# Mamba convolution: the running sum of the taps kept in the projection's PSUM banks, and the head's steps renumbered around it

## What is computed

```python
xz = jnp.einsum("bld,ed->ble", x, in_w)
xb, z = jnp.split(xz, 2, axis=-1)
xc = depthwise_conv(xb, cw)              # 4 taps, causal
xb = silu(xc + cb)
dbc = einsum("ble,re->blr", xb, xp_w)    # delta, B, C
...
v = BETA * v + mi_t                      # scan over the tokens
h = dA_t * h + v
y_t = einsum("ben,bn->be", h, C_t)
...
y = (y + dp * xb) * silu(z)
out = einsum("bld,ed->ble", y, ow)
```

## Time and profile before

| | us |
|---|---|
| median of three runs | 4340.58 |
| the profiled execution's own time | 4348.82 |
| its span (first to last instruction) | 4347.0 |
| PE busy | 3439.8 (79%) |
| DVE busy | 2853.4 (66%) |
| POOL busy | 2088.3 (48%) |
| ACT busy | 1959.2 (45%) |

### The profile page before, as it was taken

One profiled execution on the slowest core, in us unless ns is written; L12 is line 12 of the kernel. 1 busy time (PEld: TensorE's weight loads), 2 busy tenths in 40 slices (PEclk: granted clock), 3 DMA queues, 4 the chain that ended last, 5 costly groups with the idle time before them and its releaser, 6 DMA issues. The chain is left out here.

```text
span 4347.0 us, 70779 instructions
## 1 busy us (share of the span) xinstructions
PE 3439.8 (79%) x20348; PEld 2281.5 (52%) x20349; DVE 2853.4 (66%) x4863; ACT 1959.2 (45%) x4196; POOL 2088.3 (48%) x1206
## 2 busy tenths in 40 slices
PE   6888878954888888888874888888888873599980
PEld 4454545633555555555542555555555543488870
DVE  3444442335887888888865887888888867655545
ACT  1212111214666666666634666656666643233320
POOL 0101000012767767676762776767676665422216
PEclk8787877976999999999986999999999995699995
DMA  1000000011221323122221222313222115211113
GB/s 51 0 0 0 0 9 13 0 57 32 68 63 49 79 51 76 51 67 62 51 67 33 63 66 52 78 52 75 55 56 74 51 52 176 87 46 48 46 41 109
DMA packets 151529, 228.95 MB, mean 53 GB/s; under 512 B 25106, under 2 KB 83890, under 8 KB 149556
## 3 DMA queue, kind: packets, MB, share of 16 engines
q1 hardware_dynamic: 143156, 202.30, 17.4%
q0 software_dynamic: 8064, 23.08, 1.8%
HBM read 119.99 MB, written 23.59 MB: 33 GB/s over the span
## 5 line engine op out<-in xcount | busy, mean ns | idle before, releaser
L895 POOL TENSOR_TENSOR m_hc<-m_h,m_Cb 128x1024 f32<-128x1024 f32 x512 | 1212.2, 2370 | 635.2 <-DVE m_h L1019 358.1
L1019 DVE TENSOR_TENSOR_SCAN m_h<-m_dA,m_hlast,m_bank 128x256 f32<-128x256 f32 x2048 | 1348.2, 726 | 143.2 <-PE m_bank L1300 92.4
L1283 PE MATMUL m_bank<-m_hc,ident 128*128 128x512 f32 x2048 | 1145.0, 648 | 85.3 <-POOL m_hc L895 84.7
L1148 ACT ACTIVATE m_dA<-m_delta,m_rate 128x256 f32<-128x256 f32 x2048 | 881.5, 500 | 25.7 <-DVE m_h L1019 23.1
L1298 PE MATMUL m_bank<-m_M,m_U 128*128 128x128 bf16 x4096 | 607.0, 226 | 215.0 <-DVE m_h L1019 175.0
L1298 PEld LDWEIGHTS m_bank<-m_M,m_U 128*128 128x128 bf16 x4096 | 409.9, 101 | 453.0 <-DVE m_h L1019 301.6
L1300 PE MATMUL m_bank<-m_M,m_U 112*128 112x128 bf16 x4096 | 608.2, 226 | 0.0
L1300 PEld LDWEIGHTS m_bank<-m_M,m_U 112*128 112x128 bf16 x4096 | 414.8, 101 | 197.8 <-issue 169.8
L1283 PEld LDWEIGHTS m_bank<-m_hc,ident 128*128 128x128 f32 x2048 | 331.6, 200 | 138.2 <-POOL m_hc L895 102.7
L965 DVE SCALAR_TENSOR_TENSOR m_cv<-m_xpre,m_conv,m_cv 128x256 f32<-128x256 f32 x384 | 344.5, 938 | 23.1 <-ACT m_cv L1085 18.6
L1213 PE MATMUL m_bank<-m_pair,m_in 128*128 128x256 f32 x1024 | 266.5, 386 | 8.3 <-ACT m_cv L1085 4.6
(11 more groups left out here) (273 smaller groups left out, 5534.6 us busy)
## 6 DMA issues: line engine op xcount, KB each, us to landing
m_Cb<-m_c_rows SPq DMA_DIRECT2D x256, 256.0 KB, 3.3
m_M<-m_Mhi SPq DMA_DIRECT2D x128, 256.0 KB, 4.4
m_M<-m_Mlo SPq DMA_DIRECT2D x64, 256.0 KB, 3.7
m_U<-m_Uhi SPq DMA_DIRECT2D x128, 128.0 KB, 3.4
y_rows<-x_y SPq DMA_DIRECT2D x40, 256.0 KB, 2.1
m_U<-m_Ulo SPq DMA_DIRECT2D x64, 128.0 KB, 3.6
g_stage<-in_e_w SPq DMA_DIRECT2D x8, 1024.0 KB, 5.4
o_stage<-in_e_w SPq DMA_DIRECT2D x16, 512.0 KB, 4.0
```

Source lines behind the costliest of these rows:

```text
L895: nc.gpsimd.tensor_tensor(hc[:, g].rearrange("p m a t -> p m (a t)"), h[:, p % 2, 2 * g:2 * g + 2].rearrange("p m a t -> p m (a t)"), Cb[: ...
L1019: nc.vector.tensor_tensor_scan(h[:, p % 2, m, a, :], dA[:, p % 2, m, a, :], VB[m][:, a * CM:(a + 1) * CM], hlast[:, NG * p + a, m:m + 1], ...
L1148: nc.scalar.activation(dA[:, p % 2, m, a, :], delta[:, par, m, :], ACT.Exp, scale=rate[:, m, NG * p + a:NG * p + a + 1]).then_inc(s["da_do ...
L1283: last = nc.tensor.matmul(Y[g][:], net.ident[:], hc[:, g, :, a, :], start=(p == 0 and a == 0), stop=(p == NPAIR - 1 and a == NG - 1))
```

## The change

- ACT's steps 8 and 10 write the last tap plus the bias back into the projection's own bank, in place, and no longer to `cv`. A new semaphore `copy_done` makes ACT wait for its own copy to `xpre` first.
- DVE's taps k = 0 and 1 read and write that bank: `bank = xpre * w + bank`. Tap k = 2 reads it and writes `cv` in SBUF.
- So the banks are in use for longer: the z half (p4 to p7) waits for `conv_done` in place of `pre_done`, and it moves from steps 10 to 13 to steps 12 to 15.
- `OFF` becomes 11. All steps from the z half's end on (15 to 35) are renumbered by one (16 to 36) and keep their slots. Steps 0 to 9 keep their numbers and run one slot earlier: p0 to p3 in slots 27 to 30 in place of 28 to 31, ACT's steps 8 and 10 in slots 29 and 31 in place of 30 and 0. DVE's steps 11 and 13 run in slots 0 and 2 in place of 1 and 3, so both now stand ahead of the gate. The z half runs in slots 1 to 4 in place of 0 to 3.

```diff
-OFF, NG = 10, 2
+OFF, NG = 11, 2
...
-                 "z_done conv_done xb_done bc_psum xp_psum xp_done b_done dt_psum far_done exp_done square_done near_done "
+                 "z_done copy_done conv_done xb_done bc_psum xp_psum xp_done b_done dt_psum far_done exp_done square_done near_done "
...
                         dve.wait_ge(s["pre_done"], 1 + q * 2 + g + 1)
                         for k in range(TAPS - 1):
                             for m in (2 * g, 2 * g + 1):
-                                i = nc.vector.scalar_tensor_tensor(cv[:, m, :], xpre[:, m, k:k + CM],
-                                                                   conv[:, m, k:k + 1], cv[:, m, :], ALU.mult, ALU.add)
+                                tap = halves((H0, H1)[g])[:, m % 2, :]
+                                to = tap if k < TAPS - 2 else cv[:, m, :]
+                                i = nc.vector.scalar_tensor_tensor(to, xpre[:, m, k:k + CM],
+                                                                   conv[:, m, k:k + 1], tap, ALU.mult, ALU.add)
...
                         act.wait_ge(s["halo_done"], 1 + q + 1)
                         act.wait_ge(s["in_psum"], 1 + q * 4 + g + 1)
-                        nc.scalar.copy(xpre[:, 2 * g:2 * g + 2, TAPS - 1:], halves((H0, H1)[g]))
+                        nc.scalar.copy(xpre[:, 2 * g:2 * g + 2, TAPS - 1:], halves((H0, H1)[g])).then_inc(s["copy_done"], 1)
+                        act.wait_ge(s["copy_done"], 1 + q * 2 + g + 1)
                         for m in (2 * g, 2 * g + 1):
-                            last = nc.scalar.activation(cv[:, m, :], halves((H0, H1)[g])[:, m % 2, :], ACT.Identity,
+                            tap = halves((H0, H1)[g])[:, m % 2, :]
+                            last = nc.scalar.activation(tap, tap, ACT.Identity,
                                                         bias=conv_b[:, m:m + 1], scale=conv[:, m, TAPS - 1:TAPS])
                         last.then_inc(s["pre_done"], 1)
...
-                    if 6 <= at < 6 + 2 * KI:
-                        m = at - 6
+                    if 6 <= at < 6 + KI or 8 + KI <= at < 8 + 2 * KI:
+                        m = at - 6 if at < 6 + KI else at - 8
...
                         if g >= 2:
-                            pe.wait_ge(s["pre_done"], 1 + q * 2 + g - 1)
+                            pe.wait_ge(s["conv_done"], 1 + q * 2 + g - 1)
...
-                    if at == 15:
+                    if at == 16:
```

More of the change, by code:

```diff
@@ L860, in head @@
                                               ).then_inc(s["halo_done"], 1)
-                    if at == 21:
+                    if at == 22:
                         pool.wait_ge(s["b_done"], 1 + q + 1)
@@ L866, in head @@
                         matrix(q, 0)
-                    if at == 23:
+                    if at == 24:
                         matrix(q, 1)
-                    if at == 25:
+                    if at == 26:
                         matrix_low(q, 0)
-                    if at == 27:
+                    if at == 28:
                         pool.wait_ge(s["ghi_done"], 1 + q + 1)
@@ L874, in head @@
                                                 ALU.subtract).then_inc(s["glo_done"], 1)
-                    if at == 28:
+                    if at == 29:
                         pool.wait_ge(s["delta_done"], 1 + q + 1)
                         nc.gpsimd.tensor_tensor(u[:], delta[:, par], xb[:, par], ALU.mult).then_inc(s["u_done"], 1)
-                    if at == 30:
+                    if at == 31:
                         matrix_low(q, 1)
@@ L974, in head @@
                                                     ALU.max, ALU.min).then_inc(s["clamp_done"], 1)
-                    if at == 26:
+                    if at == 27:
                         dve.wait_ge(s["square_done"], 1 + q + 1)
@@ L986, in head @@
                         last.then_inc(s["delta_done"], 1)
-                    if at == 32:
+                    if at == 33:
                         for j in range(TM):
@@ L991, in head @@
                                                     ).then_inc(s["ulo_done"], 1)
-                    if at == 35:
+                    if at == 36:
                         dve.wait_ge(s["chi_done"], 1 + q + 1)
@@ L1095, in head @@
                         nc.scalar.activation(xb[:, par], cv[:], ACT.Silu).then_inc(s["xb_done"], 1)
-                    if at == 18:
+                    if at == 19:
                         act.wait_ge(s["xp_psum"], 1 + q + 1)
@@ L1099, in head @@
                         nc.scalar.copy(xp, H0[0:RANK + 2 * NS, 0:CM]).then_inc(s["xp_done"], 1)
-                    if at == 20:
+                    if at == 21:
                         act.wait_ge(s["bc_psum"], 1 + q + 1)
@@ L1103, in head @@
                                        ).then_inc(s["b_done"], 1)
-                    if at == 22:
+                    if at == 23:
                         for g in range(2):
@@ L1117, in head @@
                                              ).then_inc(s["square_done"], 1)
-                    if at == 25:
+                    if at == 26:
                         act.wait_ge(s["clamp_done"], 1 + q * 2 + 2)
                         nc.scalar.activation(u[:], delta[:, par], ACT.Exp).then_inc(s["near_done"], 1)
-                    if at == 26:
+                    if at == 27:
                         act.wait_ge(s["near_done"], 1 + q + 1)
                         nc.scalar.activation(u[:], u[:], ACT.Ln, bias=1.0).then_inc(s["ln_done"], 1)
-                    if at in (24, 27):
-                        j = (at - 24) // 3
+                    if at in (25, 28):
+                        j = (at - 25) // 3
                         act.wait_ge(s["mf_done"], 1 + q * TM + j + 1)
@@ L1128, in head @@
                         nc.scalar.copy(Mhi[:, j], Mf[:, j]).then_inc(s["mhi_done"], 1)
-                    if at == 31:
+                    if at == 32:
                         act.wait_ge(s["u_moved"], 1 + 6 * 16 * q)
@@ L1133, in head @@
                             nc.scalar.copy(Uhi[:, j, :], (H0, H1)[j][:]).then_inc(s["uhi_done"], 1)
-                    if at == 34:
+                    if at == 35:
                         act.wait_ge(s["carry_psum"], 1 + q + 1)
@@ L1217, in head @@
                             last.then_inc(s["in_psum"], 1)
-                    if at == 17:
+                    if at == 18:
                         pe.wait_ge(s["xb_done"], 1 + q + 1)
@@ L1224, in head @@
                         last.then_inc(s["xp_psum"], 1)
-                    if at == 19:
+                    if at == 20:
                         pe.wait_ge(s["xp_done"], 1 + q + 1)
@@ L1250, in head @@
                             last.then_inc(s["uT_psum"], 1)
-                    if at == 33:
+                    if at == 34:
                         pe.wait_ge(s["moved_next"], 1 + 3 * 16 * q)
```

4 lines of the change are left out of this document (2 added, 2 removed).

## The result

The changed kernel takes 4220.67 us (median of four runs, 4213.47 to 4224.86), the kernel before 4342.68 us beside it. The ratio is 0.9709 with a 95% interval of 0.9676 to 0.9742. The forecast was 4222. That the two agree to 1.3 us is partly luck: the step on the loop turns was wrong, and terms that came out larger than forecast made up for it, as the last sections show.

A forecast was written before the change was run, and what follows sets the result against it. PE was taken as close to its limit, its largest stall 4.79 us a period behind DVE's scan. Periods 114 plus loop turns 16 less serial heads 12 gave 118 us, so 4222 us; 8 in 10 between 4175 and 4290.

The forecast's parts named there:

- the step on the loop turns: Eight periods' "issue" stalls of PE at slot 2's velocity, 1.26 us each, hidden by DVE's taps: 16 us gained with clock.
- Taps in PSUM: DVE's taps with the running sum in PSUM: 0.45 us each, six in 2.7 us.
- slow taps: Rival: DVE's taps from PSUM take the scan's 0.66 us each, gaining 22 us, 4319; chance 0.13.
- The slower rival: POOL not what lengthens DVE's taps; both slow sets stand ahead of the gate: 2.6 us a period later, 4431; chance 0.05.
- DVE's chain: DVE's scans, twelve taps, then gate, then POOL: PE's accumulate step of product 1 18.6 us after slot 0's velocity starts, before 21.93.
- the stall that moves to POOL: PE's slot 6 stall: 2.8 us for POOL's product 1 in place of 4.79 for DVE's scan.
- The clock: PE's granted clock after the slot 6 stall: half of the 1.6 us lost there comes back, 0.8 a period.
- The eight stalls of 1.5 us: PE's stall in the eight periods with an "issue" stall shrinks to 1.5 us, short enough to keep the clock.
- p0 to p3 one slot earlier: PE reaches slot 0's velocity 0.86 us later, with one group less behind it; 0.3 us a period taken off the gain.
- Serial heads: Layer heads: p6, p7 and their silu now behind the taps, ACT's step 10 earlier: loss 2 x 5.7, some 12 us.
- Other edits at nothing: ACT's copy_done wait, ACT's writes to PSUM and the other moved steps: taken as costing nothing.

The follow-up runs named there:

- the run with the longer loop: Changed kernel with only VectorE's (DVE's) loop turning over four chunks instead of two: 4184.71 us, ratio 0.9629 to the kernel before.
- product 1 and `xb` first: Changed kernel, product 1 ahead of gated on POOL, x half's silu ahead of z's on ACT: 4109.81 us; with DVE's four-chunk loop too, 4113.34.

## Why the prediction came out right, and where it did not

*Taps in PSUM: right.* 0.45 us each was taken; four take 1.77 and two 0.87, 0.44 each. That the run with both inputs in SBUF in the new order (4320) has the time of the "slow taps" rival, 4319, is a coincidence: not PSUM was slow there, but SBUF. With both inputs in SBUF the taps cost 100 us against the same order with the sum in PSUM (4320 and 4221). The Trainium skill, "VectorE: DVE Perf Modes", was weighed with two statements: the rule for authors to copy PSUM to SBUF first is the wrong way round for this kernel in the new order (in the old one PSUM cost 23 us), and the errata's 65 ns for a PSUM source do not show (483 and 478 ns against 483); the measurement decides.

*The slower rival: its condition did not hold, and its price was too high.* It asked that something other than POOL lengthens the taps. Slow taps in the new order were priced at 4431 with 11.28 us a period. Where the run with both inputs in SBUF makes them slow, fewer of them lie beside a POOL product (58 of over 0.6 us, 90 before); they take 0.685 us in the mean, 8.2 us a period, and the time stays 24 us below that of before.

*DVE's chain and the stall that moves to POOL: right where DVE's loop does not turn.* V0 + 18.6 was forecast, and V0 + 18.06 stands there without a turn, V0 + 20.04 with one; the stall names L895, 2.10 and 2.54 us in the periods shown (2.8 forecast). With product 1 ahead of `gated` 69.4 us of such waits go, 2.3 a period, which shows that it was the order on POOL's queue.

*The clock: right in the mean, not in its place.* 0.8 us a period was taken, 0.92 measured, though 1.56 in layer 1 and 0.29 in layer 2. Windows of 4 us behind the stall of slot 6, in the period without a turn and in the one with it:

```profile
1869.39:1873.39 4.00, 4.00 (x13) 2.30 (x14) 2.83 (x5) 3.97 (x8) 2.19 (x1) 0.61 0.18 66
1799.60:1803.60 4.00, 4.00 (x20) 2.62 (x20) 2.82 (x5) 3.97 (x8) 3.50 (x2) 1.00 0.21 66
```

Over all 30 periods the clock in such a window was 0.50 to 0.62 every time before; now it is 1.00 in 21 and 0.50 to 0.65 in nine. So more came back there than the half that was forecast. But each period has a second stall of 2.41 us, some 45 to 54 us behind V0, and the clock behind that one fell in 8 periods before and falls in 15 now (0.50 to 0.69). The forecast had nothing on that, so its good mean is luck in part. The eight stalls of 1.5 us that were to keep the clock do not show; behind the ten of 1.68 to 1.77 us it was 1.00.

*p0 to p3 one slot earlier: right in kind.* The waits for the carry DMAs fell by 21.1 us, so of the 30 x 0.86 = 25.8 us put there 4.7 were not free, 0.16 a period instead of 0.3.

*Loop turns: wrong, the step that failed.* The step said that the turn's 1.26 us, an "issue" stall of PE, would be hidden by DVE's taps, and gave 16 us. It looked at PE's turn. That did nearly vanish (10.1 to 3.8 us), but DVE has a turn of its own, and no row that the prediction quotes names it, since it lay in idle time of DVE there. The kernel before, DVE's timeline of a period with a turn, whose V0 is 1813.96:

```profile
1816.03 2.66 DVE L1019 TENSOR_TENSOR_SCAN m_h<-m_dA,m_hlast,m_bank 128x256 f32<-128x256 f32 x4 [2.43 <-ACT m_dA L1148]
1818.60 4.19 DVE L965 SCALAR_TENSOR_TENSOR m_cv<-m_xpre,m_conv,m_cv 128x256 f32<-128x256 f32 x6
...
1826.72 1.66 DVE L1000 SCALAR_TENSOR_TENSOR m_u<-m_xb,m_skip,m_bank 128x256 f32<-128x256 f32 x4 [1.36 <-PE m_bank L1283]
```

Scan 0 has 2.43 us of idle time ahead of it there, and 2.58 in the period without a turn. In the latter DVE was through 1.44 us before V0 (1739.46 - 2.58 against 1738.32), for V0 itself waited for a carry DMA; most of a turn lies in that time. What is left of it, a scan 0 at V0 + 2.07 in place of V0 + 1.14, is gone by the end of the first six taps, V0 + 8.8 in both. The 1.36 us by which the gate waits for PE's `Y` is PE's own turn; the gate waits so in just the eight periods with PE's "issue" stall, and without a turn it does not wait. In the changed kernel DVE is through only 0.1 us before V0 in both periods shown, and its short taps leave no gap up to the gate, so the turn goes through to product 1. The prediction moved the path onto DVE and did not ask what else DVE does on it. Twelve turns at 2 to 3 us cost an estimated 24 to 36 us (2 by scan 0, 3 by the run with the longer loop), where 16 were to be gained.

*What made up for it.* Told by what PE loses, the forecast for the 30 periods was: the stall of slot 6 from 4.79 to 2.8 us, 60 in all; the carry waits, 0.86 - 0.3 each, 17; the clock, 1.1 each with the 0.3 ahead of product 1, 33; loop turns 16. That is 126 of its 130; the rest is rounding. Measured: the long stalls of slot 6, 144.4 us, are gone and some 62 behind POOL have come (140.3 in stalls of over 1.5 us at accumulate steps, 78.1 before), so 82; carry waits 21; clock 0.92 x 30, 28; "issue" 6. Two terms were at nothing in the sum: the short waits of PE behind scans fell by 12 us (175.0 - 144.4 = 30.6 before, 18.6 now), and within the periods it waits some 8.5 for taps (26.7 less twice the head's 2.76 + 0.62 + 5.73). Together 141 of the 143.7; the rest is in no wait named here. The turns' cost is inside the stall and the taps' waits.

*Serial heads: right in kind, a little low.* 2 x 5.7 forecast, 7.6 + 5.6 measured; the x projection's 4 us were 4.4.

*Other edits at nothing.* ACT's two activations in place, PSUM to PSUM, take 0.99 us where those to SBUF took 1.03.

## What to carry to other kernels

When an instruction stands still while another engine reads the same memory, look for operands that can live in another one before shortening the work: the taps got no faster here, they only stopped waiting, and that pays only if the queue order lets the next user of that memory come later. When a change moves the path onto another engine, list everything that this engine does on the new path, its loop turns too, and look for the gaps in its old timeline that have hidden them so far. After such a change read the new last wait: moving one POOL instruction and one `silu` behind what the path needs brought almost as much again as the change itself.

## What the hardware showed that was not expected

A turn of DVE's loop delays the next scan by about 2 us in this kernel (3.16 us of idle time instead of 1.21), and the rows put that down to the last semaphore; the longer loop showed whose it is. The same turn is worth 3.0 us a period in the changed kernel, by eight turns fewer, and 1.7 to 2.0 us from V0 to V0 (69.2 to 69.5 against 67.5) with product 1 and `xb` first.

DVE can read and write the same PSUM bank in a multiply-add at 483 ns for 128x256 fp32, with the spread of all 256 within 460 to 492 while POOL is at work.
